# A four-layer graph network on one core: the first layer's attention weights as a third block of the dense builder

## The chip, the cores and the metric

The kernel is written for one NeuronCore of a Trainium2 chip and runs on one core. The metric is the device time of the run in microseconds. A core has TensorE (matrix products, with a separate queue for weight loads), VectorE, ScalarE, GpSimd and SyncE; the last, ScalarE and GpSimd issue DMA transfers.

## The reference, cut to what matters

The graph has 3125 nodes of 64 features and 100,000 edges sorted by target, with a relation type and a weight each. Four layers are applied, each to `relu(layernorm(x))` and added to `x`:

```python
edge_index = stack([src, dst])
h = maximum(layernorm(x), 0);  x = x + L0(h, ..., src, dst, edge_type)
h = maximum(layernorm(x), 0);  x = x + L1(h, edge_index, ...)
h = maximum(layernorm(x), 0);  x = x + L2(h, edge_weight, src, dst)
h = maximum(layernorm(x), 0);  x = x + L3(h, edge_index, ...)

# L0: attention with one head; what is changed is how the last sums are made
e = leaky_relu(concat([h[src], h[dst], emb_rel[etype]]) @ attn_w1 @ attn_w2)
ex = exp(e - segment_max(e, dst)[dst])
a = ex / segment_sum(ex, dst)[dst]
agg = segment_sum(a[:, None] * h[src], dst)
out = relu(where(deg > 0, agg, h) + h @ loop_weight)

# L1: sums of x[dst] @ W_msg over src, by counts of the pairs (src, dst)
# L2: twice  h = segment_sum((h * norm)[src] * w[:, None], dst) * norm
# L3: attention with 8 heads over the edges and one loop per node, then a feed-forward block
```

## The kernel before

Nodes stand as 25 blocks of 125 on 125 partitions (`NB`, `NP`), edges as 784 columns of 128 (`C`, `P`). Node features of a layer are `Hn` (125 x 25 x 64).

**Dense blocks.** Layers L1 and L2 use dense matrices, source by target: for each pair of nodes the number of edges and the sum of their weights. They are built by `dense_block`, one target block of 125 after another, 25 in all. A block's targets are cut into 42 windows of 3 targets, and a window's edges stand in one row of 128; the windows go in 7 parts of 6 (`PARTS`, `QB`). An edge is written as a one-hot row of its source's low digit (0 to 124, `hot(half, 0, W)`, L1651) and a one-hot row of 75 values (`CW`), target in the window times source's high digit (L1650). The second is multiplied by the edge weight, which is split into three bf16 parts, so that their sum keeps fp32 (L1655). TensorE multiplies the first (125 columns as the stationary operand) with counts and first weight part (150 columns, L1096), and with the other two parts (150 columns, L1098), which land in two accumulators. ScalarE copies counts and the first weight accumulator to SBUF (`counts_part`, L799), VectorE adds the second (`weights_part`, L1662, two parts later). Windows with more than 128 edges have overflow rows (26 in all), which `overflow` works off in the second part of the next block: VectorE makes the hot rows, TensorE multiplies (L1108, L1109), VectorE adds into the block (L1687 to L1690). Then ScalarE stores counts and weights (`store`), the counts as whole rows of 12,500 bytes, the weights transposed by target block in pieces of 500 bytes. The two block buffers (`wides`) lie in `big` and `arena`; the first part of a block waits for the stores of the block two before (`blk_out0`, `blk_out1`).

```python
act.dma_start(d_cnt[b], wide_c).then_inc(S[f"blk_out{u}"], 16)
act.dma_start(d_wgt[:, :, b * NP:(b + 1) * NP].rearrange("h p m -> p h m"), ...)
```

**First layer.** GpSimd gathers a feature row for every edge (`tiles`, L652: 784 indirect transfers of 128 rows for L0, and 784 for L3), SyncE stashes them in DRAM in 98 pieces (`stash`), ScalarE reloads these (`reload`). The edge look-up on TensorE and VectorE (L1052 to L1059, L1612 to L1619, 196 steps) gives the scores; `softmax0` scans them into attention weights; the weights go to DRAM (`d_al0`), and GpSimd gathers them as 7 tables (`block_rows`, L658). Then 816 steps follow (`l0_steps`, L989, and L1850): VectorE makes a 128 x 125 matrix of target marks times attention weight, and TensorE multiplies it with 128 gathered rows. Every second step has a filler matmul of 512 columns (L992). `step_targets` and `step_rows` prepare the tables.

**Order.** Histogram of the edges (`hist`: 784 matmuls of 125 columns stationary and 100 streamed, L1029), edge look-up, dense blocks, softmax, steps of L0, counts (L1, L1167 and L1175), two turns of sums (L2), then look-up, softmax, 984 positions of steps and the feed-forward block of L3. Each engine runs its own program in this order and meets the others at semaphores. In a turn of sums the 25 source blocks are read from `d_wgt` by SyncE, and each is multiplied in 7 groups of 500 columns with `T1[:, hi, :]` as the stationary operand (L1196). The result has features on partitions: ScalarE copies it (`sums_out`), TensorE transposes it back in 25 pieces.

## Time and profile before

| | us |
|---|---|
| runs, median of 3 | 3795.6 |
| lowest and highest run | 3776.2, 3814.1 |
| span of the profiled execution | 5607.6 |
| busy in it: TensorE, weight loads | 2765.6, 2175.0 |
| busy: VectorE, ScalarE, GpSimd | 2436.0, 473.0, 1797.6 |
| mean granted TensorE clock in it | 0.614 of 2.4 GHz |

The profiled execution is one execution under the hardware profiler, and here it is much longer than the runs. Every row of the trace comes from it; the change is timed by runs without the profiler. In a table by stretches a row gives start and end, the length, then for TensorE, weight loads, VectorE, ScalarE and GpSimd the busy time with the number of instructions in parentheses, then the granted clock, the share of the DMA engines that was busy, and GB/s. In a timeline a row gives the start, the length, the engine, the line, the operation, output and inputs, and in brackets the idle time before it with what ended it. Rows of the groups by line give the busy time and the mean in ns of one instruction. A matmul's length in the trace overlaps the next one's, so pitches are read from starts.

### The profile page before, as it was taken

To read this page: it belongs to the slowest core of one execution; us is meant where nothing else is said; L and a number is where in the kernel's file an instruction comes from. 1 tells how busy PE (TensorE), PEld (TensorE's weight loads), DVE (VectorE), ACT (ScalarE), POOL (GpSimd) and SP (SyncE) were. 2 spreads that over 40 slices of the span, in tenths; PEclk is the share of its full clock that TensorE was granted. 3 is DMA by queue.
4 is the path that set the end of the run, shared out by engine and by line. 5 is a ranking of instruction groups with operands and counts; after the bars stand their busy time and mean duration, and the time that the engine had idled before them with its cause. 6 is when DMAs were issued, how large, how long until landed. Compare 5 with 4: busy or idle time off the path is not lost.

```text
span 5607.6 us, 46533 instructions
## 1 busy us (share of the span) xinstructions
PE 2765.6 (49%) x14416; PEld 2175.0 (39%) x14458; DVE 2436.0 (43%) x4207; ACT 473.0 (8%) x909; POOL 1797.6 (32%) x1742
## 2 busy tenths in 40 slices
PE   2085022122678885989898500004770001059995
PEld 1083000000157774979733400004660001059983
DVE  4068221111677776970101500006999800035565
ACT  0000000000022331003200100001220110000000
POOL 3705777777100001000000777771000077720000
PEclk8555555555555555989999655557995555555556
DMA  3102222222236665314476121110000123102210
GB/s 109 52 1 61 58 75 62 71 62 65 85 82 140 138 144 155 109 49 160 177 269 220 44 52 49 46 48 10 0 0 23 70 80 73 49 15 66 63 35 23
DMA packets 246489, 433.22 MB, mean 77 GB/s; under 512 B 140538, under 2 KB 142311, under 8 KB 231895
## 3 DMA queue, kind: packets, MB, share of 16 engines
q10 hardware_dynamic: 126001, 172.60, 12.0%
q1 hardware_dynamic: 64102, 198.46, 10.0%
q0 software_dynamic: 56256, 60.51, 5.8%
q8 instruction: 72, 1.18, 0.1%
q14 instruction: 58, 0.48, 0.0%
HBM read 280.32 MB, written 150.98 MB: 77 GB/s over the span
## 4 chain that ended last, share of the span: by engine, by line
PE 35%; issue 25%; another core or an unknown queue 17%; DVE 10%; POOL 9%; DMA 2%; ACT 1%; DVEq 0%; SPq 0%; ACTq 0%; POOLq 0%
POOL ring L652 8%; PE PS L1272 7%; PE PS L1196 5%; PE PS L1096 4%; PE PS L1098 4%; PE PS L989 3%; PE PS L1029 3%; PE PS L1167 3%; PE PS L992 2%; PE PS L1175 1%; DVE s_ring L1612 1%; DVE s_ring L1613 1%; PE PS L1270 1%; PE PS L1290 1%
## 5 line engine op out<-in xcount | busy, mean ns | idle before, releaser
L652 POOL DMA_INDIRECT ring<-d_h,idx_lin x1568 | 1579.1, 1007 | 598.6 <-issue 519.4
L1272 PE MATMUL PS<-arena,s_ring 128*128 x1968 | 432.5, 414 | 198.1 <-issue 198.1
L1096 PE MATMUL PS<-qa 128*125 128x150 bf16 x1050 | 412.3, 393 | 107.0 <-DVE arena L1662 46.1
L1929 DVE TENSOR_TENSOR big<-PS,big 128x800 f32<-128x800 f32 x196 | 193.8, 989 | 619.5 <-issue 335.7
L1272 PEld LDWEIGHTS PS<-arena,s_ring 128*128 128x128 f32 x1968 | 439.8, 330 | 9.2 <-issue 1.1
L1221 PE MATMUL PS<-big 128*125 128x128 bf16 x784 | 134.0, 300 | 618.5 <-issue 449.2
L1098 PE MATMUL PS<-qa 128*125 128x150 bf16 x1050 | 401.2, 382 | 0.0
L1059 PE MATMUL PS<-s_ring,arena 81*128 81x512 bf16 x196 | 121.6, 621 | 561.0 <-issue 353.3
L1221 PEld LDWEIGHTS PS<-big 128*125 128x125 bf16 x784 | 106.9, 209 | 664.8 <-issue 456.6
L671 POOL DMA_INDIRECT d_fa<-asd,start_i x25 | 50.2, 2010 | 889.5 <-DVEq L1323 882.2
L1231 PE MATMUL PS<-big,arena 125*128 125x200 bf16 x2352 | 271.6, 272 | 118.3 <-ACT arena L900 100.9
L1096 PEld LDWEIGHTS PS<-qa 128*125 128x125 bf16 x1050 | 262.5, 250 | 136.0 <-DVE qa L1655 96.0
L1979 DVE TENSOR_TENSOR big<-big,PS 128x512 f32 x123 | 84.6, 688 | 510.1 <-remote 225.3
L1059 PEld LDWEIGHTS PS<-s_ring,arena 81*128 81x128 bf16 x196 | 20.6, 105 | 686.9 <-issue 399.8
L1231 PEld LDWEIGHTS PS<-big,arena 125*128 125x128 bf16 x2352 | 234.7, 111 | 127.7 <-issue 67.8
L1196 PE MATMUL PS<-big,arena 125*64 125x500 f32 (+1 forms) x700 | 267.2, 544 | 25.7 <-DVEq L1323 25.7
L1029 PE MATMUL PS<-s_ring 128*125 128x100 bf16 x784 | 183.3, 411 | 171.4 <-DVE s_ring L1455 110.7
L1098 PEld LDWEIGHTS PS<-qa 128*125 128x125 bf16 x1050 | 264.3, 252 | 0.0
L1850 DVE TENSOR_SCALAR s_ring<-iota_row,arena 128x125 f32<-128x125 f32 x816 | 244.7, 345 | 27.8 <-issue 20.0
L658 POOL DMA_INDIRECT arena<-d_al,tk_i x7 | 6.6, 943 | 773.8 <-DMA d_al<-qa 772.0
L1029 PEld LDWEIGHTS PS<-s_ring 128*125 128x125 bf16 x784 | 180.6, 325 | 173.8 <-DVE s_ring L1455 112.3
L989 PEld LDWEIGHTS PS<-arena,s_ring 128*125 128x125 f32 x1632 | 234.2, 192 | 20.0 <-issue 4.3
(445 smaller groups left out, 4572.2 us busy)
## 6 DMA issues: line engine op xcount, KB each, us to landing
big<-d_wgt SPq DMA_DIRECT2D x50, 1562.5 KB, 7.2
d_stash<-ring SPq DMA_DIRECT2D x196, 256.0 KB
arena<-d_stash ACTq DMA_DIRECT2D x196, 256.0 KB
big<-d_cnt SPq DMA_DIRECT2D x25, 1562.5 KB, 6.5
ring<-d_h,idx_lin POOLq DMA_INDIRECT x1568
d_cnt<-big ACTq DMA_DIRECT2D x13, 1562.5 KB, 5.5
d_wgt<-big ACTq DMA_DIRECT2D x13, 1562.5 KB, 15.7
d_cnt<-arena ACTq DMA_DIRECT2D x12, 1562.5 KB, 5.4
```

The source lines that it names most:

```text
L652: pool.indirect_dma_start(ring[:, HALF * h + s, :], None, table, bass.IndirectOffsetOnAxis(ap=idx_lin[:, CH * i + s:CH * i + s + 1], axis= ...
L989: nc.tensor.matmul(PS[0:NP, bass.ds(to[s], D)], s_ring[:, (j * CH + s) % RING, 0:NP], arena[:, bass.ds(at[s], D)], start=False, stop=False ...
L1029: mm = nc.tensor.matmul(bank(7, NP, 4 * NB), free(s_bf[:, 0:1], [[HALF, NP]], h * W * HALF + s_), free(h_bf[:, 0:1], [[HW * HALF, 4], [HAL ...
L1096: nc.tensor.matmul(bank(3 * half + s // 2, NP, 2 * CW, at), lhs, hot_step(half, s, W, 2 * CW), start=(s % 2 == 0), stop=False, skip_group_ ...
L1098: mm = nc.tensor.matmul(bank(3 * half + s // 2, NP, 2 * CW, at + CW), lhs, hot_step(half, s, W + 2 * CW, 2 * CW), start=False, stop=False, ...
L1167: mm = nc.tensor.matmul(bank(0, NP, D, hi * D), blk_t[:, hi, 0:NP], t_row[:, slot_no, :], start=False, stop=False, skip_group_check=True)
L1196: mm = nc.tensor.matmul(bank(g, D, n), T1[:, hi, :], blk_in[:, slot_no, GW * g:GW * g + n], start=(hi == 0), stop=(hi == NB - 1))
L1221: mm = nc.tensor.matmul(bank(4 + j, NP, P, s * P), free(look_hot[:, 0:1], [[CB, NP]], j * CB * W + s), ident_bf, start=True, stop=True)
L1231: mm = nc.tensor.matmul(bank(2 * j, P, HN, s * (BANK // 2)), look_t[0:NP, j, s * P:(s + 1) * P], src_parts[:, r * HN:(r + 1) * HN], start= ...
L1272: mm = nc.tensor.matmul(PS[:, bass.ds(place[s] + j % SUMS * BANK, D)], marks[:, j % 2, s, :], arena[:, bass.ds(at[s], D)], start=False, st ...
L1850: v_.tensor_scalar(s_ring[:, k % RING, 0:NP], iota_row[:, 0:NP], dstl[:, k:k + 1], alpha0[:, k:k + 1], ALU.is_equal, ALU.mult).then_inc(S[ ...
L1929: v_.tensor_tensor(picked.rearrange("p (s h k) -> p s h k", s=CB, h=H), free(PS[:, 0:1], [[BANK // 2, CB], [NB, H], [1, NB]], 2 * j * BANK ...
```

## The change

The attention weights of L0 become a third block of the dense builder. They are split into three bf16 parts like the edge weights, and each window now has three matmuls with the same stationary operand, now 128 columns wide: the first streams counts, first weight part and first attention part (225 columns), the other two the second and third parts of both (150 columns each), into the same accumulator. VectorE's add goes; ScalarE copies all three quantities. Counts and weights are stored in one transfer, `d_blk[b]`, as whole rows of 25,000 bytes. The attention block stays in SBUF: TensorE multiplies it with `Hn` in 25 fp32 products of 125 x 64 (`agg_products`), five behind each of the last five parts of the next block, and ScalarE copies the sum (`agg_rows`).

So the softmax now stands ahead of the dense blocks, and the attention weights are gathered into the windows' rows (16 gathers, then 16 transposes). The gathers, stash, reloads, tables and steps of L0 go. The blocks now lie with the source on partitions and the target in the columns, so the sums of L2 are made with a slice of the block as the stationary operand: 625 products of 125 x 64 in a turn, whose result needs no copy and no transpose. The histogram's stationary operand, too, has 128 columns.

```diff
-    W = NP + 1
+    W = P
     CW = WN * NB
-    HOT = QB * (W + 4 * CW)
+    HOT = QB * (W + 7 * CW)
...
-        d_cnt = dram("d_cnt", (NB, P, N))
-        d_wgt = dram("d_wgt", (NB, P, N))
-        d_h0 = dram("d_h0", (N, D))
+        d_blk = dram("d_blk", (NB, P, 2 * N))
...
-            nc.gpsimd.memset(arena[:, 0:2 * N], 0.0)
...
-            tiles(0, d_h0, 0, 18)
...
-            tiles(0, d_h0, 18, 40)
+            pool.wait_ge(S["alpha_out"], 16)
+            for g in range(DG):
+                pool.indirect_dma_start(arow[:, g * P:(g + 1) * P], None, d_al0,
+                                        bass.IndirectOffsetOnAxis(ap=tk5_i[:, g:g + 1], axis=0)).then_inc(S["arows_in"], 16)
...
-            block_rows(d_dst, dstl, "drow0_in")
-            tiles(0, d_h0, 40, NCH)
-            pool.wait_ge(S["alpha_out"], 16)
-            block_rows(d_al0, alpha0, "rows_in")
...
-                for q in range(2):
+                for q in range(3):
                     last = nc.scalar.activation(free(blk[:, 0:1], [[NP, NB], [WN, n], [1, WN]], q * N + p * QB * WN),
-                                                free(PS[0:NP, 0:1], [[1, NB], [BANK // 2, n], [NB, WN]], half * 3 * BANK + q * CW), ACT.Copy)
+                                                free(PS[:, 0:1], [[1, NB], [BANK // 2, n], [NB, WN]], half * 3 * BANK + q * CW), ACT.Copy)
...
-                    act.dma_start(d_cnt[bass.ds(2 * i + b, 1)].rearrange("o p m -> p (o m)"), wide_c).then_inc(S[f"blk_out{u}"], 16)
-                    act.dma_start(d_wgt[:, :, bass.ds(2 * NP * i + b * NP, NP)].rearrange("h p m -> p h m"),
-                                  wide_w.rearrange("p (h m) -> p h m", h=NB)).then_inc(S[f"blk_out{u}"], 16)
+                to = d_blk[b] if i is None else d_blk[bass.ds(2 * i + b, 1)].rearrange("o p m -> p (o m)")
+                act.dma_start(to, wides[u][:, 0:2 * N]).then_inc(S[f"blk_out{u}"], 16)
+
+            def agg_rows(i, n):
+
+                act.wait_ge(S["agg_done"], n + 3 if i is None else 2 * i + (n + 3))
...
+                nc.scalar.activation(to, bank(7, NP, D), ACT.Copy).then_inc(S["agg_out"], 1)
...
                 for s in range(QB):
-                    at = s % 2 * (BANK // 2)
-                    lhs = hot_step(half, s, 0, NP)
-                    nc.tensor.matmul(bank(3 * half + s // 2, NP, 2 * CW, at), lhs, hot_step(half, s, W, 2 * CW),
+                    at = half * 3 * BANK + s * (BANK // 2)
+                    lhs = hot_step(half, s, 0, W)
+                    nc.tensor.matmul(PS[:, at:at + 3 * CW], lhs, hot_step(half, s, W, 3 * CW),
                                      start=(s % 2 == 0), stop=False, skip_group_check=True)
-                    mm = nc.tensor.matmul(bank(3 * half + s // 2, NP, 2 * CW, at + CW), lhs, hot_step(half, s, W + 2 * CW, 2 * CW),
-                                          start=False, stop=False, skip_group_check=True)
+                    for r in range(1, 3):
+                        mm = nc.tensor.matmul(PS[:, at + CW:at + 3 * CW], lhs, hot_step(half, s, W + (2 * r + 1) * CW, 2 * CW),
+                                              start=False, stop=False, skip_group_check=True)
...
+            def agg_products(i, n, first, end):
...
+                for hi in range(first, end):
+                    mm = nc.tensor.matmul(bank(7, NP, D), wides[n % 2][0:NP, 2 * N + hi * NP:2 * N + (hi + 1) * NP], Hn[:, hi, :],
+                                          start=(hi == 0), stop=(hi == NB - 1), skip_group_check=True)
...
+                    if p >= 2 and not first:
+                        agg_products(i, b - 1, NB // 5 * (p - 2), NB // 5 * (p - 1))
...
-            l0_steps()
...
-                    for g in range(GROUPS):
-                        n = min(GW, N - GW * g)
-                        mm = nc.tensor.matmul(bank(g, D, n), T1[:, hi, :], blk_in[:, slot_no, GW * g:GW * g + n],
-                                              start=(hi == 0), stop=(hi == NB - 1))
+                    for s in range(NB):
+                        mm = nc.tensor.matmul(bank(0, NP, D, hi * D), blk_in[:, slot_no, s * NP:(s + 1) * NP], T1[:, s, :],
+                                              start=(s == 0), stop=(s == NB - 1))
...
-            for k in range(K):
-                v.wait_ge(S["agg_mm"], k + 1)
-                v_.tensor_scalar(s_ring[:, k % RING, 0:NP], iota_row[:, 0:NP], dstl[:, k:k + 1], alpha0[:, k:k + 1],
-                                 ALU.is_equal, ALU.mult).then_inc(S["s_ready"], 1)
...
+                v_.tensor_tensor(to_w, hits, at_w[:, :, :, bass.ds(k, QB)], ALU.mult)
+                v_.tensor_tensor(to_a, hits, at_a[:, :, :, bass.ds(k, QB)], ALU.mult).then_inc(S["one_ready"], 1)
```

**Order on TensorE, inside the loop of the dense blocks.** Before, the end of one part and the start of the next (L1090 is the wait's register, L1096 and L1098 the two products of a window):

```order
L1096 MATMUL PS<-qa 125x150
L1098 MATMUL PS<-qa 125x150
L1096 MATMUL PS<-qa 125x150
L1098 MATMUL PS<-qa 125x150
L1090 REGISTER_ALU
L1096 MATMUL PS<-qa 125x150
L1098 MATMUL PS<-qa 125x150
L1096 MATMUL PS<-qa 125x150
L1098 MATMUL PS<-qa 125x150
```

After, the same place (L1015 and L1018 are the three products of a window, L1041 those of the attention block):

```order
L1015 MATMUL PS<-qa 128x225
L1018 MATMUL PS<-qa 128x150 x2
L1041 MATMUL PS<-Hn,big 125x64 x5
L1010 REGISTER_ALU
L1015 MATMUL PS<-qa 128x225
L1018 MATMUL PS<-qa 128x150 x2
L1015 MATMUL PS<-qa 128x225
L1018 MATMUL PS<-qa 128x150 x2
```

A third product stands in each window, and five fp32 products stand between two parts.

**Order on VectorE, from the look-up to the first part of the blocks.** Before (L1629 is the last instruction of the placing of overflow rows, L1633 to L1638 split the tables, L1650 begins the hot rows):

```order
L1629 CAST pos_c<-PS 7x128
L1633 CAST big<-qa 128x2048
L1634 TENSOR_SCALAR big<-qa 128x2048
L1636 CAST big<-qa 128x2048
L1638 TENSOR_TENSOR qa<-qa,big 128x2048
L1636 CAST big<-qa 128x2048
L1638 TENSOR_TENSOR qa<-qa,big 128x2048
L1636 CAST big<-qa 128x2048
L1639 CAST qa<-iota_row 128x756
L1650 TENSOR_TENSOR qa<-qa,big 128x450
L1651 TENSOR_TENSOR qa<-qa,big 128x756
L1655 TENSOR_TENSOR qa<-qa,big 128x1350
```

After (L1579 is the last multiply of the softmax, L1675 to L1671 the tables of keys and weights, those with PS the attention weights):

```order
L1579 TENSOR_TENSOR qa<-qa,big 128x784
L1675 CAST s_ring<-qa 128x2048
L1676 TENSOR_SCALAR s_ring<-qa 128x2048
L1669 CAST big<-qa 128x2048
L1671 TENSOR_TENSOR qa<-qa,big 128x2048
L1669 CAST big<-qa 128x2048
L1671 TENSOR_TENSOR qa<-qa,big 128x2048
L1669 CAST big<-qa 128x2048
L1669 CAST qa<-PS 128x2048
L1671 TENSOR_TENSOR qa<-PS,qa 128x2048
L1669 CAST qa<-qa 128x2048
L1671 TENSOR_TENSOR qa<-qa 128x2048
```

The softmax's end now stands ahead of the tables, and five instructions for the attention weights follow them.

**Order on GpSimd, its queue of gathers up to the steps of the last layer.** Before (L652 feature rows, L681 node values to the edge list, L686 rows of the windows, L658 targets and attention weights by step, L700 tables of the last layer):

```order
L652 DMA ring<-d_h,idx_lin 128x64 x144
L681 DMA d_fa<-nfl,start_i 100352x1 x25
L686 DMA big<-d_dense,tk_i 128x384 x16
L652 DMA ring<-d_h,idx_lin 128x64 x176
L658 DMA arena<-d_dst,tk_i 128x128 x7
L652 DMA ring<-d_h,idx_lin 128x64 x464
L658 DMA arena<-d_al,tk_i 128x128 x7
L700 DMA dst<-d_dst,tk_i 128x128 x7
L700 DMA dst<-d_dst,tk_i 88x128
```

After (L643 gathers the attention weights into the windows' rows):

```order
L634 DMA d_fa<-nfl,start_i 100352x1 x25
L639 DMA big<-d_dense,tk_i 128x384 x16
L643 DMA big<-d_al,tk_i 128x128 x16
L652 DMA dst<-d_dst,tk_i 128x128 x7
L652 DMA dst<-d_dst,tk_i 88x128
L627 DMA d_fa<-asd,start_i 100352x8 x25
```

784 gathers of feature rows and 14 tables are gone, and 16 gathers of attention weights stand in their place.

## Rows read from the trace of the kernel before

**Rows 1.** Table by stretches, one row for each stage that is used.

```profile
85.00:298.00 213.00, 38.37 (x161) 35.05 (x160) 14.78 (x34) 3.11 (x7) 137.57 (x144) 0.52 0.27 80
298.00:454.00 156.00, 156.00 (x681) 156.00 (x682) 113.79 (x255) 0.00 (x0) 0.00 (x0) 0.50 0.00 1
...
545.00:1422.00 877.00, 168.38 (x306) 32.81 (x305) 186.52 (x430) 0.00 (x0) 659.70 (x642) 0.50 0.26 67
1422.00:1572.00 150.00, 118.69 (x242) 25.81 (x242) 122.21 (x255) 1.08 (x2) 6.65 (x7) 0.50 0.26 81
...
1594.00:2160.00 566.00, 462.30 (x2152) 432.74 (x2152) 419.06 (x883) 174.06 (x375) 0.00 (x0) 0.50 0.62 136
...
2220.00:2474.00 254.00, 254.00 (x2022) 233.88 (x2021) 244.42 (x816) 1.28 (x1) 0.95 (x1) 0.97 0.32 89
...
2772.00:3060.00 288.00, 275.76 (x745) 101.74 (x745) 11.62 (x9) 6.21 (x14) 0.00 (x0) 0.96 0.71 262
...
3127.00:3836.00 709.00, 97.95 (x644) 79.06 (x644) 88.32 (x118) 23.79 (x40) 515.85 (x504) 0.53 0.19 47
3836.00:4215.00 379.00, 274.36 (x2492) 237.68 (x2492) 351.26 (x471) 93.35 (x156) 0.00 (x0) 0.96 0.00 0
...
4493.00:4931.00 438.00, 40.02 (x180) 36.97 (x183) 17.18 (x24) 16.44 (x16) 334.31 (x331) 0.51 0.25 62
4931.00:5418.00 487.00, 430.55 (x1934) 425.10 (x1972) 243.90 (x346) 0.00 (x0) 13.49 (x13) 0.50 0.15 41
```

**Rows 2.** Groups by line: L1612 in 545:1300 and 1422:1572, L1059 in all.

```profile
L1612 DVE TENSOR_SCALAR s_ring<-arena,tk 125x512 bf16<-125x512 uint8 x44 | 20.9, 476 | 0.0
...
L1612 DVE TENSOR_SCALAR s_ring<-qa,tk 125x512 bf16<-125x512 uint8 x42 | 20.1, 477 | 0.2
...
L1059 PEld LDWEIGHTS PS<-s_ring,arena 81*128 81x128 bf16 x196 | 20.6, 105 | 686.9 <-issue 399.8 <-DVE s_ring L1619 280.9 <-remote 6.2
```

**Rows 3.** Timeline of one part of a dense block, and of its overflow row.

```profile
1802.08 0.39 DVE L1650 TENSOR_TENSOR qa<-qa,big 128x450 bf16<-128x450 bf16 x1
...
1802.38 0.55 DVE L1651 TENSOR_TENSOR qa<-qa,big 128x756 bf16<-128x756 bf16 x1
...
1802.61 0.26 PEld L1096 LDWEIGHTS PS<-qa 128*125 128x125 bf16 x1
...
1802.81 0.25 PEld L1098 LDWEIGHTS PS<-qa 128*125 128x125 bf16 x1
1802.85 0.86 DVE L1655 TENSOR_TENSOR qa<-qa,big 128x1350 bf16<-128x1350 bf16 x1
...
1803.62 0.62 DVE L1662 TENSOR_TENSOR arena<-arena,PS 125x450 f32<-125x450 f32 x1
...
1817.52 0.21 DVE L1664 TENSOR_TENSOR arena<-arena,PS 125x50 f32<-125x50 f32 x1
...
1822.30 0.39 DVE L1650 TENSOR_TENSOR qa<-qa,big 128x450 bf16<-128x450 bf16 x1 [0.49 <-DVE arena L1690]
```

**Rows 4.** Timeline of the tables, and of the hand-over to the steps.

```profile
1582.60 1.23 DVE L1633 CAST big<-qa 128x2048 bf16<-128x2048 f32 x1 [0.17 <-DVE pos_c L1629]
...
1586.38 2.29 DVE L1638 TENSOR_TENSOR qa<-qa,big 128x2048 f32<-128x2048 f32 x1
...
2203.70 0.94 POOL L658 DMA_INDIRECT arena<-d_al,tk_i  x1 [0.30 <-issue]
...
2219.74 2.39 DVE L1850 TENSOR_SCALAR s_ring<-iota_row,arena 128x125 f32<-128x125 f32 x9 [19.98 <-issue]
```

**Rows 5.** Table by stretches of 4 us in the count stage.

```profile
2540.00:2544.00 4.00, 4.00 (x21) 4.00 (x20) 0.00 (x0) 1.01 (x3) 0.00 (x0) 0.50 0.00 0
...
2552.00:2556.00 4.00, 4.00 (x38) 3.92 (x37) 0.00 (x0) 1.60 (x4) 0.00 (x0) 1.00 0.00 0
```

**Rows 6.** DMA issues: KB each, then us to landing; the block stores.

```profile
d_cnt<-big ACTq DMA_DIRECT2D x13, 1562.5 KB, 5.5
d_wgt<-big ACTq DMA_DIRECT2D x13, 1562.5 KB, 15.7
```

## What I expect, and why

> **What bounds the kernel now.** I read the table by stage first, then short timelines inside the stages. The profiled execution lasts 5607.6 us, the runs 3796 us. So something in the trace is not in the runs, and it has to be found before any sum. Four stretches carry it, and in all four GpSimd issues row gathers. In 85 to 298 us TensorE does 161 matmuls; in the next 156 us it does 681 [rows 1]. The edge look-up does 430 VectorE instructions in 877 us, then 255 in 150 us [rows 1]. The look-up of the last layer gets through 40 groups (ScalarE's count) in 709 us, then 156 in 379 us [rows 1]. The last layer's steps: 24 VectorE instructions in 438 us, then 346 in 487 us [rows 1]. At the free pace the four would hold about: 104 histogram matmuls at 0.229 = 24 us; some 84 look-up steps at 3 x 150/255 = 1.76 us or less (short timelines without a gather show less; I take 1.5) plus 60 us of tables = about 185; 40 x 2.43 = 97; and for the last, where the gathers themselves pace the steps, an end some 420 us earlier. Stall: 189 + 692 + 612 + 420 = 1913 us. 5608 - 1913 = 3695 us, 3% below the median of the runs. So I read the stalls as a thing of the profiled execution, nearly absent from the runs, and make the sum against 3796 with the unstalled stretches. What bounds the runs is then a chain of stages: histogram, edge look-up, dense blocks, softmax, the 816 steps, counts, two sums, last layer. The first turn of gathers (784 of about 1.3 us, so 1.0 ms) ran beside look-up and dense blocks, which hold about 0.9 ms with the histogram; it was on no chain of its own by more than a little.
>
> **Removed.** (1) The steps of the first layer, 2220 to 2474 us, TensorE and VectorE both over 95% busy [rows 1]: -254 us. Their gathers, stash stores and reloads were hidden in the runs and go at 0. In the profiled execution they take their two stalls with them, 189 + 692 = 881 us. The other bound: of the 101 us by which my stall-free figure misses the runs, half may be this turn's, so up to -50. (2) The second table set in the middle of the look-up, about 52 small VectorE instructions at some 0.2 us: -10 us.
>
> A page's rule would add a gain. While GpSimd gathers, does it slow VectorE itself? The equality instruction L1612 takes 476 ns on average beside the gathers (545 to 1300 us) and 477 without them (1422 to 1572 us) [rows 2]; I count 0. The Trainium skill ("SBUF — State Buffer", Who interferes with whom) says that VectorE and GpSimd share a port pair by an exclusive lock, held for a whole instruction; by that the look-up's VectorE work would speed up too. The trace does not bear it out for this form.
>
> **Histogram.** The stationary operand goes from 125 to 128 columns. It now runs 681 matmuls in 156 us, 0.229 each, 1.83 us for a step of 8, while VectorE is busy 113.8 us for 85 steps, 1.34 each [rows 1]. Loads of 128 bf16 columns take 105 ns in the trace (81x128, at 1.2 GHz) [rows 2], loads of 125 columns 250 ns [rows 3]. In the dense stage pairs of load and matmul follow each other at 0.20 us although 150 columns stream in 0.125 us at 1.2 GHz [rows 3], so the load sets that pitch. With the short load the histogram becomes VectorE's: 98 x (1.83 - 1.37) = -45 us. Bounds: 0 if the load stays slow, -48.
>
> **Before the blocks.** The softmax (40 us) moves ahead of them whole. From its last multiply to the first step, at 2219.74, VectorE stood idle for 20 us, with 7 gathers of 0.94 + 0.30 us [rows 4]. Now 16 gathers: +11 us; 9 more transposes: +2; three casts of 1.23 and two subtractions of 2.29 for the alpha parts: +8.3 [rows 4]. The tables of keys and edge weights (five of 1.23, two of 2.29, 11 us) now lie behind the gathers: -11; rounding for the last iota, -4. Sum +6 us.
>
> **The blocks, now 566 us** [rows 1], 22.6 us each. VectorE per part: 0.30 + 0.47 + 0.77 start to start for the hot rows [rows 3], and 0.53 for the add, which goes; the second product costs another 0.77. So 2.31 us against 2.07. TensorE per part: 18 pairs instead of 12, 6 x (225 + 150 + 150) = 3150 columns, 2.63 us at 1.2 GHz and 1.31 at 2.4, if loads hide; before, 12 x 0.205 = 2.46. In five of seven parts come 5 fp32 products of 125x64. Such products are two matmuls each (816 steps and 408 fillers are 2040, of which the trace has 2022 [rows 1]); the count stage (125x64 products and transposes, fp32 as well) does 21 matmuls in 4 us at the low clock and 38 at the high one [rows 5], so 0.19 or 0.105 each, 2.0 or 1.05 us per part. The overflow row (one per block, 26 in all) holds VectorE from the last add to 1822.30, about 4.6 us [rows 3]; now TensorE is less behind: 4.2. A block is then
>
> - high clock: VectorE decides, 7 x 2.31 + 4.2 = 20.4 us; 25 of them 510, with a start of 10, 520 us;
> - low clock: TensorE decides, 7 x 2.63 + 25 x 2 x 0.19 + 3.7 of wait after the overflow row = 31.6 us; 790 us, plus 10.
>
> Which clock? Today the stage is at 0.50 with TensorE busy 82% [rows 1], with gaps at every part. The changed one leaves it no gap for five parts of seven at the low clock. The count stage, without gaps, ran at 0.50 from 2520 to about 2548 and then rose [rows 5]; the edge look-up (3 matmuls of 512 columns a step, 79% busy) never rose [rows 1, 5]; the last look-up stayed at 0.96 with 72% busy [rows 1]. I take the rise, with some falling back at the overflow waits: 22.8 us a block, 570 us, +4 us. The whole-row store helps here: 500-byte pieces took 15.7 us, whole rows of the same size 5.5 [rows 6], and ScalarE waited for that store at each block's first part. 3.1 MB in whole rows is about 2 x 5.5 = 11 us, against 11.7 us between its issue and the wait. If it takes 13, VectorE's margin covers half, and the stage grows by some 20 us.
>
> **After the blocks.** The last overflow row, 25 products, two copies and the wait for the last store: +12 us. Then counts as before: their clock fell before them too.
>
> **The two sums.** Both turns take 288 us [rows 1]: 350 matmuls of up to 500 columns each, then ScalarE's copies, transposes and a few VectorE instructions. Now each has 625 products of 125x64, 1250 matmuls at 0.107 = 134 us at the high clock, no copies, no transposes; but such a stream began with 28 us at the low clock (21 matmuls in 4 us [rows 5]), which costs 14. With 6 and 16 us between and behind them, 134 + 14 + 6 + 134 + 16 = 304: +16 us. At the low clock throughout: 1250 x 0.19 = 238, +210 us for both. DMA: 1.56 MB per 5.4 us is the load of today.
>
> **Sum:** -254 - 10 - 45 + 6 + 4 + 12 + 16 = -271. 3796 - 271 = 3525 us, ratio 0.929. In the profiled execution another 881 us go: a span near 4460.
>
> **Rivals.**
> 1. The clock stays low in the blocks: 3525 + 800 - 570 = 3755 us, 1% below before. For it: the edge look-up, bf16 and one-hot rows as here, dense in columns and never up. Against: it uses 81 to 125 rows of the array, and the new blocks hold dense fp32 products. The Trainium skill ("TensorE: Matmul & The Clock Gate", What's actually happening) says that sustained activity releases the throttle; by that this rival falls, but the look-up's 0.50 speaks against a simple reading.
> 2. Slower: the 128-column load is not fast here, where the columns lie 12 bytes apart (in the row of 105 ns they lie side by side). Then 18 pairs at 0.205 are 3.69 us a part; a block 7 x 3.69 + 9.5 + 3.7 = 39 us, 976 us, the histogram saves nothing: 3525 + 406 + 45 = 3976 us. It decides against the change from the pitch at which the blocks use up the 271 us: (841/25 - 13.2)/126 = 0.162 us a pair. If it comes with the high clock, 0.105 a pair gives 1.9 + 1.05 us a part and 3635 us.
> 3. The sums stay at the low clock: 3525 + 194 = 3720 us. For it: the steps of the last layer, 64-column fp32 as well, ran at 0.50 for 487 us. Against: they pause at each step, the count stage did not.
> 4. The change does less than it says: the gathers were co-critical or not, the hand-over is longer, the store is waited for. Upwards 3575, downwards 3470.
>
> **Numbers.** Forecast as summed 0.57; its own range, with the dense stage between 520 and 640 and the 50 us, 3440 to 3610. Rival 1: 0.14. Rival 2 at the low clock 0.10, at the high one 0.04. Rival 3: 0.07. Rival 4: 0.08, inside the first range. Range 3440 to 3790, which leaves out rival 2 and what lies below. A measurement of this kernel tells about 1% from no change. Faster by over 1% (under 3758): 0.57 + 0.08 + 0.07 + 0.04 and most of half of rival 1, less what each may miss: 0.77. Within 1%: 0.11. Slower: 0.12.
>
> **What would show it.** No stall in the histogram and the edge look-up, which takes about 300 us in one piece. Histogram steps of 1.37 us. Loads of 128 columns near 0.11 us in the blocks and in the histogram. Blocks of 20 to 24 us with a granted clock mostly at 1.0; at 0.50 they would be near 32. No wait of ScalarE for the block store. The sums at 134 to 150 us each with the clock at 1.0 after the first 30 us. If blocks take over 33 us, or sums over 230, the forecast is wrong in that term; if the runs fall by far more than 300 us, the first turn's gathers cost the runs what I gave to the profiled execution alone.

## The result, and the profile of the changed kernel

The change made the kernel slower: 4266.5 us (median of 4 runs, 4257.1 to 4274.8) against 3792.1 (4 runs, 3776.2 to 3814.1), ratio 1.126 with an interval of 1.121 to 1.131. I had forecast 3525 us.

One fact has to stand ahead of the comparison. A job is a set of kernels that were run together on one chip, the kernel before always among them, and the jobs are of two kinds: in one the kernel before takes about 3790 us in every run, in the other about 5600. The execution of [rows 1] is of the second kind, so the stalls that I read out of it do not come from the profiler. They do not follow the chip's number either: chip 3 had stalls (two jobs) and chip 10 had none, but number 2 stands for a job with stalls and, four minutes later, for one without. The profile of the changed kernel (span 4263.3 us) has no stalls. A stall-free profile of before came out of an experiment: the kernel before without the first turn of gathers, 3784.4 us there, ratio 0.9985 to before. Its stages are the ones to compare with.

The table by stretches of the changed kernel (start:end, length, then busy time and count of TensorE, weight loads, VectorE, ScalarE, GpSimd, then granted clock, DMA share, GB/s): histogram, edge look-up, dense blocks, counts, the two sums, the last layer from its gathers on.

```profile
102.00:256.00 154.00, 153.53 (x781) 105.28 (x780) 130.59 (x292) 0.00 (x0) 0.00 (x0) 0.50 0.00 1
321.00:637.00 316.00, 284.02 (x587) 62.90 (x585) 300.96 (x648) 0.00 (x0) 20.23 (x14) 0.50 0.32 99
741.00:1832.00 1091.00, 994.84 (x4411) 655.08 (x4412) 462.12 (x876) 254.64 (x570) 0.00 (x0) 0.50 0.16 70
1904.00:2115.00 211.00, 211.00 (x1884) 208.94 (x1884) 0.00 (x0) 93.08 (x197) 0.00 (x0) 1.00 0.47 167
2136.00:2667.00 531.00, 524.71 (x2500) 524.54 (x2500) 11.62 (x9) 0.00 (x0) 0.00 (x0) 0.50 0.39 142
2708.00:4263.00 1555.00, 943.50 (x5828) 838.68 (x5827) 1077.45 (x1151) 171.45 (x272) 979.80 (x867) 0.67 0.24 66
```

The same view of the kernel before without its first gathers, stall-free; its fourth row is the steps of the first layer:

```profile
102.00:282.00 180.00, 179.85 (x784) 179.61 (x784) 130.95 (x296) 0.00 (x0) 11.21 (x128) 0.50 0.11 43
345.00:702.00 357.00, 286.05 (x587) 63.13 (x587) 324.27 (x714) 0.00 (x0) 131.41 (x661) 0.50 0.44 149
733.00:1290.00 557.00, 461.04 (x2148) 432.07 (x2149) 414.65 (x869) 173.03 (x372) 0.00 (x0) 0.50 0.58 137
1358.00:1608.00 250.00, 250.00 (x2036) 230.91 (x2035) 242.59 (x812) 1.28 (x1) 0.00 (x0) 0.99 0.31 90
1664.00:1883.00 219.00, 218.86 (x1892) 216.60 (x1890) 0.10 (x1) 93.79 (x198) 0.00 (x0) 0.96 0.44 161
1903.00:2184.00 281.00, 272.08 (x723) 97.41 (x724) 11.62 (x9) 3.11 (x7) 0.00 (x0) 0.97 0.73 268
2232.00:3785.00 1553.00, 931.10 (x5787) 838.41 (x5828) 1078.41 (x1151) 171.49 (x272) 978.57 (x867) 0.67 0.23 66
```

| from | before | after | difference | forecast |
|---|---|---|---|---|
| histogram | 180 | 154 | -26 | -45 |
| end of histogram to first dense product (look-up; softmax now in it) | 451 | 485 | +34 | +56 |
| dense blocks | 557 | 1091 | +534 | +4 |
| from there to the counts (softmax and steps, now the last products) | 374 | 72 | -302 | -302 |
| counts | 219 | 211 | -8 | 0 |
| two sums, to the last layer | 349 | 593 | +244 | +16 |
| last layer | 1553 | 1555 | +2 | 0 |

The differences add up to +478 us, the spans (3785.9 and 4263.3) differ by 477. The forecast's column adds up to its -271. The 60 us of softmax and hand-over leave the fourth row (-254 - 60 + 12 = -302) and come into the second (-10 + 60 + 6 = +56). The dense blocks and the sums took 778 us more between them where I had 20. Of the other terms, the histogram gained 19 us less than forecast, and the look-up's row came out 22 us better: the look-up itself gained 41 us (316 instead of 357) where I had counted 10, and what follows it took back a part.

A part of a dense block in the changed kernel, rows of its timeline (start, length; several instructions in one row have their count behind x):

```profile
1240.61 0.48 PE L1015 MATMUL PS<-qa 128*128 128x225 bf16 x1
...
1240.91 0.59 PE L1018 MATMUL PS<-qa 128*128 128x150 bf16 x2
...
1241.32 0.48 PE L1015 MATMUL PS<-qa 128*128 128x225 bf16 x1
1241.32 0.13 PEld L1018 LDWEIGHTS PS<-qa 128*128 128x128 bf16 x1
...
1242.74 2.18 PE L1041 MATMUL PS<-Hn,big 125*125 125x64 f32 x10
...
1243.06 0.39 DVE L1691 TENSOR_TENSOR qa<-qa,s_ring 128x450 bf16<-128x450 bf16 x1 [3.83 <-PE PS L1018]
...
1244.71 0.48 PE L1015 MATMUL PS<-qa 128*128 128x225 bf16 x1
...
1248.97 2.19 PE L1041 MATMUL PS<-Hn,big 125*125 125x64 f32 x10
```

The load is short, as forecast (0.13 us against 0.25 [rows 3]). Still 225 columns take 0.30 us and 150 take 0.20, so a window takes 0.71 us: 1.33 ns a column where 1.2 GHz would need 0.83. A part is six windows and ten matmuls of the attention block, 4.26 + 1.97 = 6.23 us. VectorE waits 3.83 us in each, and a block takes 1091 / 25 = 43.6 us.

### The profile page after: what moved, and what is told of

It is laid out like the page before. It is cut to its first block, busy times and chain, and to the rows that moved or that the text cites. A ratio compares the mean times of both kernels' runs of the same rounds, so it can differ in the third digit from the quotient of the medians.

```text
span 4263.3 us, 48040 instructions
## 1 busy us (share of the span) xinstructions
PE 3222.3 (76%) x16493; PEld 2491.6 (58%) x16494; DVE 2219.0 (52%) x3326; ACT 545.1 (13%) x1092; POOL 1078.1 (25%) x959
## 4 chain that ended last, share of the span: by engine, by line
PE 53%; POOL 23%; DVE 10%; issue 9%; DMA 3%; ACT 1%; SPq 0%; DVEq 0%; ACTq 0%; POOLq 0%
POOL ring L614 20%; PE PS L1109 12%; PE PS L1018 10%; PE PS L1015 7%; PE PS L1041 6%; PE PS L931 4%; PE PS L1081 3%; PE PS L1182 2%; PE PS L1089 2%; DMA qa<-d_code 2%; PE PS L954 1%; POOL nmx L620 1%; DVE arena L1877 1%; POOL d_fb L627 1%; PE PS L955 1%
## 5 line engine op out<-in xcount | busy, mean ns | idle before, releaser
L614 POOL DMA_INDIRECT ring<-d_h,idx_lin x784 | 850.7, 1085 | 250.7 <-issue 250.7
L1018 PE MATMUL PS<-qa 128*128 128x150 bf16 x2100 | 616.1, 383 | 0.0
L1015 PE MATMUL PS<-qa 128*128 128x225 bf16 x1050 | 505.7, 482 | 105.7 <-DVE qa L1697 105.7
L1109 PE MATMUL PS<-arena,big 125*125 125x64 f32 x2500 | 525.5, 416 | 26.3 <-DVEq L1233 20.0
L1109 PEld LDWEIGHTS PS<-arena,big 125*125 125x125 f32 x2500 | 525.1, 332 | 26.5 <-DVEq L1233 26.5
L1018 PEld LDWEIGHTS PS<-qa 128*128 128x128 bf16 x2100 | 270.4, 129 | 248.8 <-issue 176.3
L652 POOL DMA_INDIRECT dst<-d_dst,tk_i x8 | 7.6, 950 | 1171.6 <-DVEq L1233 1169.5
L1015 PEld LDWEIGHTS PS<-qa 128*128 128x128 bf16 x1050 | 148.5, 141 | 183.0 <-DVE qa L1697 99.9
L1822 DVE TENSOR_REDUCE qa<-big 128x800 f32 x196 | 193.2, 986 | 28.3
L749 ACT ACTIVATE big<-PS 128x450 f32<-128x450 f32 (+1 forms) x273 | 128.9, 548 | 497.4 <-PE PS L1018 497.4
L749 ACT ACTIVATE arena<-PS 128x450 f32<-128x450 f32 (+1 forms) x252 | 119.1, 549 | 406.0 <-PE PS L1018 406.0
L954 PE MATMUL PS<-s_ring,arena 125*81 125x512 bf16 x196 | 127.5, 650 | 54.6 <-DVE s_ring L1520 53.9
```

What stands on the lines that cost most here:

```text
L614: pool.indirect_dma_start(ring[:, HALF * h + s, :], None, table, bass.IndirectOffsetOnAxis(ap=idx_lin[:, CH * i + s:CH * i + s + 1], axis= ...
L749: last = nc.scalar.activation(free(blk[:, 0:1], [[NP, NB], [WN, n], [1, WN]], q * N + p * QB * WN), free(PS[:, 0:1], [[1, NB], [BANK // 2, ...
L1015: nc.tensor.matmul(PS[:, at:at + 3 * CW], lhs, hot_step(half, s, W, 3 * CW), start=(s % 2 == 0), stop=False, skip_group_check=True)
L1018: mm = nc.tensor.matmul(PS[:, at + CW:at + 3 * CW], lhs, hot_step(half, s, W + (2 * r + 1) * CW, 2 * CW), start=False, stop=False, skip_gr ...
L1109: mm = nc.tensor.matmul(bank(0, NP, D, hi * D), blk_in[:, slot_no, s * NP:(s + 1) * NP], T1[:, s, :], start=(s == 0), stop=(s == NB - 1))
L1822: v_.tensor_reduce(qa[:, bass.ds(CB * H * g, CB * H)], picked.rearrange("p (s k) -> p s k", k=NB), AX_X, ALU.add).then_inc(S["look_sum"], 1)
```

## Experiments

Stage times are first to last product of the stage; only they are compared between jobs. Whole times are compared within one job. The kernels of the last two parts (both remedies, the stalls) ran 4 to 10 times in a job, and their times are medians; each of the others ran once. What the expectations call a chip with or without stalls is a job of that kind. Line numbers are each kernel's own; the first matmul of a window is the one that streams 225 columns.

**The streamed operand side by side.**

```diff
+            return free(hots[:, 0:1], [[1, n]], h * HOT + at * QB + j * n)
...
-                    nc.tensor.matmul(PS[:, at:at + 3 * CW], lhs, hot_step(half, s, W, 3 * CW),
+                    nc.tensor.matmul(PS[:, at:at + 3 * CW], lhs, hot_stream(half, s, W, 3 * CW),
```

> The changed kernel, with one thing other: the streamed operand of the three products of a window is read from neighbouring columns (2 bytes apart) instead of columns 12 bytes apart. What is streamed is then not the window's own columns, so the dense blocks hold other numbers. Theory A (the stream of columns 12 bytes apart sets the pitch: in the profile of the changed kernel 150 columns take 0.20 us and 225 take 0.30, 1.33 ns a column, at a granted clock of 0.50): pitches fall to 0.125 and 0.19 us at 1.2 GHz, a part's 18 matmuls from 4.23 to about 2.7 us, the dense stage from 1117 to about 850 us, the time from 4267 to about 4000. Theory B (the load of the stationary operand sets the pitch, as my forecast had it for 125 columns): no change, 4267 within 1%. If the clock rises as well, the stage falls below 700 us.

Measured: dense stage 593 us at a clock of 0.81, in a job with stalls. Theory A held, and the clock rose too, with TensorE busy only 81% of the time. The row of the stage, then a window where the clock stood at 1.00, in which 225 columns take 0.10 us, 0.44 ns each:

```profile
741.00:1334.00 593.00, 481.20 (x4413) 458.54 (x4414) 461.12 (x875) 255.27 (x570) 0.00 (x0) 0.81 0.30 130
```

```profile
999.87 0.26 PE L1018 MATMUL PS<-qa 128*128 128x225 bf16 x1
999.97 0.29 PE L1021 MATMUL PS<-qa 128*128 128x150 bf16 x2
```

**The stationary operand side by side** (`lhs` read with step 1 instead).

> The changed kernel with the stationary operand (not the streamed one) of the windows' products read from neighbouring columns; the blocks then hold other numbers. Read by the dense stage, first to last product (1091 us in the changed kernel, 593 with the streamed operand side by side). Theory A (the stream's 12-byte steps set the pitch): still 1091 us, pitches 0.20 and 0.30 us. Theory B (loads count too): shorter pitches, a stage under 1050 us. TensorE's granted clock stays at 0.50 by A.

Measured: 1084 us at 0.50, 4268.2 us in all (before 3795.6 beside it). The step of the loads costs next to nothing here.

```profile
744.00:1828.00 1084.00, 987.91 (x4411) 649.21 (x4412) 462.02 (x875) 255.09 (x570) 0.00 (x0) 0.50 0.17 71
```

**Other steps of the streamed operand** (2 or 4 elements instead of 6 in `hot_step`'s place).

> The changed kernel with the streamed operands read at other steps: 4 bytes for the 225 columns and for the first 150, 8 bytes for the second 150; the blocks then hold other numbers. If a column costs 0.111 ns for each byte of step, as 1.33 ns at 12 bytes would have it, 4 bytes cost 0.44 ns and the clock sets the pitch (0.42 or 0.83 ns a column), and 8 bytes cost 0.89 ns: 0.133 us for 150 columns at either clock. If instead any step above 2 bytes costs the same, the pitches stay at 0.30 and 0.20 us and the stage at 1091 us. By the first the stage is near 600 us with the clock at 0.8 or above.

Measured: 595 us at 0.92, 3769.3 us in all. The table row, then two windows of the timeline at the high clock:

```profile
744.00:1338.00 594.00, 496.32 (x4407) 483.56 (x4405) 460.93 (x874) 255.91 (x570) 0.00 (x0) 0.92 0.30 129
```

```profile
1020.39 0.28 PE L1018 MATMUL PS<-qa 128*128 128x225 bf16 x1
1020.51 0.37 PE L1021 MATMUL PS<-qa 128*128 128x150 bf16 x2
1020.70 0.29 PE L1018 MATMUL PS<-qa 128*128 128x225 bf16 x1
```

At 4 bytes 225 columns take 0.12 us, 0.53 ns each, not far from the 0.44 of neighbouring columns. The two of 150, one at 4 and one at 8 bytes, take 0.19 to 0.20 together, so the one at 8 bytes takes about 0.12, an estimated 0.8 ns a column. Steps of 12 bytes cost 1.33 ns. In the changed histogram, where the columns lie 16 bytes apart, eight loads of 128 columns go by in 1.28 us with products of 100 columns between them, about 1.6 ns a column if the stream is what holds them there, which no run tested. From 8 bytes on the cost grows about with the distance, some 1.6 to 1.8 ns for each 16 bytes passed. The Trainium skill ("SBUF — State Buffer", Door 1: The DMA port swizzle, the note on cachelines) says that SBUF has lines of 16 bytes, that each access to a new line costs, and that two hits on a line are enough for full bandwidth. The steps of 12 bytes agree with that; the step of 8 bytes, two hits on a line, does not, with about 0.8 ns a column at the high clock. I had not weighed that rule. By it the stream of [rows 3] would have been a rival to the load for what sets the pitch of 0.20 us.

**A filler matmul behind each window.**

```diff
+                    mm = nc.tensor.matmul(bank(3 * half + s // 2, P, BANK), ones_bf[:, 0:P], zero_bf[:, 0:BANK], start=False, stop=False, skip_group_check=True)
```

> The changed kernel with one more matmul behind the three of each window: 512 columns of zeros with ones as the stationary operand, added to the window's own bank, so the result stays. Theory A (the clock is low in the blocks because the stream is too thin, and more streamed columns raise it): granted clock 1.0, a part's PE work (4.23 + 6 x 0.43) / 2 = 3.4 us or less, the dense stage about 28 us a block, 700 us, the time about 3850. Theory B (the clock stays at 0.50 whatever TensorE streams here, as in the edge look-up of the first layer): a part grows by 6 x 0.43 = 2.6 us, the stage by 450 us, the time to about 4720.

Measured: neither. The clock rose to 0.94, as theory A said, but the stage took 1217 us, 126 more than without fillers. Table row, then the timeline where the clock stood at 1.00 (L1021 is the filler):

```profile
741.00:1959.00 1218.00, 1115.03 (x5360) 659.00 (x5461) 462.94 (x877) 255.03 (x570) 0.00 (x0) 0.94 0.15 63
```

```profile
1247.41 0.46 PE L1015 MATMUL PS<-qa 128*128 128x225 bf16 x1
1247.69 0.59 PE L1018 MATMUL PS<-qa 128*128 128x150 bf16 x2
1248.10 0.40 PE L1021 MATMUL PS<-zero_bf,ones 128*128 128x512 bf16 x1
1248.33 0.46 PE L1015 MATMUL PS<-qa 128*128 128x225 bf16 x1
```

The streams 12 bytes apart take 0.28 us for 225 columns and 0.205 for 150 at the high clock too, against 0.30 and 0.205 at the low one. So twice the clock hardly changes their pace; only fillers and fp32 products went faster. The high clock alone would not have given the forecast's 20.4 us a block.

**Without the products of the attention block** (24 of 25 left out).

> The changed kernel without 24 of the 25 fp32 products of each attention block (the first layer's sums are then missing). A block has 240 fewer matmuls at 0.22 us each for pairs: 24 x 0.44 = 10.6 us a block if TensorE alone sets the pace, 265 us of the stage's 1091. If their place were covered by VectorE's work: under 50 us. The clock stays at 0.50 if the windows' stream decides it; if the fp32 products hold it down, it rises.

Measured: 862 us at 0.50, so -229 us; 4037.0 us in all. TensorE paces alone, and these products cost 24 x 2 x 0.19 = 9.1 us a block. They did not hold the clock down.

```profile
742.00:1604.00 862.00, 766.15 (x3269) 418.60 (x3267) 461.42 (x874) 255.47 (x570) 0.00 (x0) 0.50 0.21 89
```

**The kernel before, streamed operand side by side.**

> The kernel before with the streamed operand of its dense blocks read side by side (the blocks then hold other numbers). My forecast took the load of 125 columns for what sets the pitch of 0.20 us. If that was right: pitch and clock stay, the dense stage stays near 557 us. If the 12-byte step set it there too: pitch down to what load and 150 columns allow (0.125 us at the low clock if loads hide), TensorE's part 1.5 to 1.9 us, VectorE sets the pace, stage 510 to 540 us, granted clock up if TensorE then streams densely enough.

Measured: 518 us instead of 557, clock 0.50 in both, pitch 0.175 us instead of 0.20. The row of the stage and two starts, 0.17 us apart:

```profile
1593.00:2111.00 518.00, 395.44 (x2147) 376.98 (x2147) 410.92 (x870) 172.89 (x372) 0.00 (x0) 0.50 0.62 147
```

```profile
1805.74 0.38 PE L1101 MATMUL PS<-qa 128*125 128x150 bf16 x1
...
1805.91 0.38 PE L1099 MATMUL PS<-qa 128*125 128x150 bf16 x1
```

Both views were partly right. The 12-byte step set 0.20. What is left, 0.175, is more than the 0.125 of 150 columns at 1.2 GHz, and the load of 125 columns is the likely reason; no run changed it. VectorE, busy for 411 of the 518 us, kept the gain small.

**The roles in the sums swapped back.**

```diff
-                        mm = nc.tensor.matmul(bank(0, NP, D, hi * D), blk_in[:, slot_no, s * NP:(s + 1) * NP], T1[:, s, :],
+                        mm = nc.tensor.matmul(bank(hi // 4, D, NP, hi % 4 * NP), T1[:, s, :], blk_in[:, slot_no, s * NP:(s + 1) * NP],
```

> The changed kernel with the roles in the two sums swapped back: T1 (64 columns) is the stationary operand, each 125 x 125 slice of a block is streamed, ScalarE copies the seven banks and TensorE transposes the 25 pieces, as before. Theory A (64 streamed fp32 columns behind a load of 125 keep the clock low; 125 streamed behind a load of 64 raise it): granted clock near 1.0, both turns about 300 us instead of 500, the time about 4065. Theory B (the low clock comes from what ran before or from the small pieces as such): clock 0.50; 78125 columns at the low clock are 270 us a turn, the time about 4300.

Measured: 287 us for both turns, clock 0.97. Theory A held, and what ran before the sums was the same. The same 2500 matmuls (and 25 transposes), with 125 columns streamed behind loads of 64 instead of 64 behind loads of 125:

```profile
2144.00:2431.00 287.00, 278.08 (x2525) 277.52 (x2524) 11.62 (x9) 3.11 (x7) 0.00 (x0) 0.97 0.72 263
```

**Fillers in the sums**, one of 512 columns behind every fifth product, then behind each.

> The changed kernel with a filler matmul of 512 bf16 columns (into a bank that nobody reads) behind every fifth product of the two sums, 250 in all. Theory A (more streamed columns raise the clock): 134 + 125 x 0.21 = 161 us a turn at the high clock, both about 340 us instead of 500, the time about 4110. Theory B (it doesn't): 250 x 0.43 = 107 us more, the time about 4375.

> The changed kernel with a filler matmul of 512 bf16 columns behind every product of the two sums (1250; with one behind every fifth the clock stayed at 0.50 and the sums took 611 us). If more streamed columns raise the clock: near 1.0, and a turn is 1250 x 0.107 + 625 x 0.21 = 267 us, both about 550. If the clock stays low: 1250 x 0.20 + 625 x 0.43 = 519 us a turn, both about 1060.

Measured: 611 us at 0.50 with 250 fillers, 492 us at 0.99 with 1250 (532 at 0.50 without). The two rows:

```profile
2137.00:2748.00 611.00, 605.00 (x2750) 580.48 (x2751) 11.67 (x10) 0.00 (x0) 0.00 (x0) 0.50 0.34 124
```

```profile
2136.00:2629.00 493.00, 486.55 (x3751) 446.83 (x3751) 11.75 (x10) 0.00 (x0) 0.00 (x0) 0.99 0.42 154
```

TensorE is busy 99% of the time in all three, so the busy time of a profile does not tell which clock was granted. With 250 fillers the clock stayed low and they cost 79 us; with 1250 it rose, and the stage was 40 us shorter although it held more work. The Trainium skill ("TensorE: Matmul & The Clock Gate", What's actually happening) says that activity releases the throttle; read as the busy time of a profile, that does not hold here (524.71 of 531 us busy at 0.50).

**Hot rows in pairs.** VectorE writes the streamed rows so that the windows of a pair stand side by side; a step's columns are then 4 bytes apart.

```diff
-            return free(hots[:, 0:1], [[QB, n]], h * HOT + at * QB + j)
+            return free(hots[:, 0:1], [[2, n]], h * HOT + j // 2 * HG + at * 2 + j % 2)
```

> The changed kernel with the hot rows laid out in pairs of windows: a step's columns are 4 bytes apart instead of 12; all results as in the reference. VectorE writes runs of two instead of six elements, and makes six multiplications of 450 elements a part instead of two of 1350. If the step is the cause and 4 bytes are short enough: TensorE's part falls as with neighbouring columns, the dense stage to 600 to 660 us (VectorE's part is 0.30 + 0.47 + 6 x 0.30 = 2.57 us if runs of two keep its rate), clock at 0.8 or above. If VectorE loses its rate in short runs: 3918 elements at about 1 ns, 4.2 us a part, 30 a block, 820 us.

Measured: 644 us at 0.85, 3822.2 us in all (before 3795.6). The blocks hold the right numbers here, so the gain of the run with neighbouring columns did not come from its other numbers. In this kernel a slip of naming also took another row of constants in the last layer's layer norm; no stage read here is touched by it, and the later kernels are without it. At the low clock 225 columns 4 bytes apart take 0.19 us, 0.83 ns each, so there the clock sets the pace again:

```profile
1004.88 0.39 PE L1018 MATMUL PS<-qa 128*128 128x225 bf16 x1
...
1005.07 0.46 PE L1021 MATMUL PS<-qa 128*128 128x150 bf16 x2
```

VectorE's multiplications keep their rate in runs of two (0.30 us for 450 elements), its two comparisons do not quite: 462 and 670 ns on average instead of 394 and 552.

**Both remedies.** Pairs and swapped roles; then with the stationary rows left in runs of six.

> The changed kernel with both remedies, all results as in the reference: hot rows in pairs of windows (columns of the streamed operand 4 bytes apart) and T1 as the stationary operand of the two sums. If the two causes are independent, the dense stage is 644 us (1091 in the changed kernel) and the sums 287 (532): 4267 - 447 - 245 = 3575 us, ratio to the kernel before 0.94. If one remedy only moves the wait, it is above 3700.

> As the kernel with both remedies, but only the streamed rows are laid out in pairs; the stationary ones stay in runs of six, columns 12 bytes apart, where VectorE writes them in 0.47 us instead of 0.57. If the stationary operand's step costs TensorE nothing (the run with side-by-side loads says so), VectorE's 0.10 us in each of 175 parts is gained: 17 us less than with all rows in pairs, about 3560. If it costs at the high clock: no gain, or a loss.

Measured, in a job with stalls: 4530.4 us, ratio 0.8075 (0.804 to 0.811), and 4513.5 us, 0.8046 (0.801 to 0.808). Dense stage 669 and 648 us, sums 287 in both. The gain of the second over the first, 17 us, is the expected one, but the intervals overlap, and the dense stage of the first took 669 us here and 644 in the run before it with the same code for the blocks (clock 0.81 and 0.85). A difference of 20 us in such a stage shows nothing.

> The kernel with both remedies and only the streamed rows in pairs, once more. On the chip without stalls the stage times (dense blocks 648, sums 287 us, against 1091 and 532 of the changed kernel) give 4267 - 443 - 245 = 3579 us, ratio to the kernel before 0.944. On the chip with stalls: 4513 us, 0.805, as before.

> The kernel with both remedies (streamed rows in pairs, T1 as the stationary operand of the sums), for the chip without stalls: 4267 - 443 - 245 = 3579 us, ratio 0.944. If the job falls on the chip with stalls: 4515 us, 0.805, as twice before.

Measured: 4522.3 us, 0.8063 (0.804 to 0.809) with stalls; without them 3580.7 us, ratio 0.9472 (0.9448 to 0.9496) to the kernel before at 3785.6. So the version with both remedies beats the kernel before in both kinds of jobs, and the changed kernel too (5209.0 us beside the 4522.3, and 1.126 to before where this one has 0.947). Its dense stage and sums without stalls:

```profile
742.00:1384.00 642.00, 492.18 (x4414) 466.48 (x4415) 515.65 (x1571) 254.90 (x570) 0.00 (x0) 0.84 0.28 120
1686.00:1973.00 287.00, 277.94 (x2525) 277.48 (x2525) 11.62 (x10) 3.11 (x7) 0.00 (x0) 0.97 0.72 263
```

**The stalls.**

> The changed kernel, unaltered. On the chip with stalls: the runs of this kernel with one thing altered there (4970 us with 245 us less in the sums, 5331 with 126 more in the blocks, 5283 with 79 more in the sums) give 5204 to 5215 us, so the change is FASTER there than the kernel before, ratio 0.93. On the chip without stalls 4267 us, ratio 1.125. By the rival (the stalls have nothing to do with the gathers that the change removes) the ratio is about 1.1 on both.

> The kernel before with the 784 gathers of the first layer left out (each is a small GpSimd memset of zeros; stash, reloads and steps stay, so the first layer's sums are zero). On the chip without stalls my forecast has the gathers hidden: 3795 us within 50. If they slow the look-up or the blocks there: 100 us or more less. On the chip with stalls: two stalls of 189 and 692 us go, 5600 - 881 = about 4720 us.

> The kernel before without the first layer's 784 gathers, for the chip without stalls: 3795 us within 50 if they are hidden there, as the forecast had it; 3700 or less if they slow the look-up and the blocks. On the chip with stalls: 4733 us, as before.

Measured: in a job with stalls the changed kernel takes 5209.0 us, ratio 0.930 (0.927 to 0.933), so there the same change is a gain. The kernel before without its first gathers takes 4733.2 us there, 871 less than 5604.3 (expected 881), and 3784.4 against 3785.6 without stalls. The look-up of the last layer in the changed kernel, first in a job with stalls, then without:

```profile
3000.00:3100.00 100.00, 8.00 (x44) 5.98 (x44) 4.62 (x6) 1.79 (x3) 75.73 (x74) 0.50 0.18 51
```

```profile
3000.00:3100.00 100.00, 73.00 (x674) 63.14 (x674) 93.31 (x127) 25.13 (x42) 74.63 (x78) 0.98 0.20 52
```

GpSimd gathers at the same pace in both; TensorE gets through 44 matmuls where it otherwise does 674. What the engines wait for is not shown (the waits name "issue" and "remote", up to 45 us each). What makes one job stall and another not stays open: with number 2 in both kinds, the runs do not show that it is the chip, although the expectations name it so.

## Why the forecast was wrong

**What held.** That the stalls hang on the gathers, and their size: 881 us for the first turn, and 4733 us shows 871. I had them as a thing of the profiled execution, though, and they are in every run of some jobs. That the gathers cost nothing without stalls: ratio 0.9985. The upper bound of 50 us for them was not needed. Steps, softmax and hand-over: -302 us where I had -302. The short load of 128 columns. The store: 8.8 us for 3.1 MB, and ScalarE waits for TensorE, not for it.

**The step that failed first** is the sentence on the pitch: 150 columns stream in 0.125 us at 1.2 GHz, "so the load sets that pitch". The 0.20 us fitted both a load of 0.25 us that overlaps, and a stream that is slow by itself. I took the one without asking what else could give it, although the columns' distance stood in the code and I used it in the slower rival, on the wrong operand. With 1.33 ns a column a part is 3150 x 1.33 = 4.2 us at either clock, where I had 2.63 or 1.31. That is 7 x 1.6 = 11 us a block above my low-clock case, 280 us in all. The runs show this step wrong: with the stream side by side and the loads as they were the stage fell from 1091 to 593 us, with the loads side by side it stayed at 1084.

**The second is the clock**, in the blocks and in the sums. I took its rise in the count stage as a sign for any dense fp32 stream. The sums ran at 0.50 for 532 us with TensorE 99% busy, and the dense stage for 1091 us with 91%. The count stage was no such stream by itself. It holds a transpose of 125 streamed columns for every two matmuls of 64:

```profile
L1167 PE MATMUL PS<-big 125*125 125x64 f32 x1208 | 157.3, 276 | 0.0
L1175 PE MATMUL PS<-ident,big 125*125 125x125 f32 x615 | 97.6, 292 | 0.0
```

The new sums have the matmuls of 64 alone, and with 125 columns streamed instead they ran at 0.97. Whether the transposes are what let the count stage rise was not tested.

Rival 1 and rival 3 came true together, and I had priced each alone: 800 - 570 = 230 us and 194 us. With the stream's 280 that is 704 us; measured were 530 + 228 = 758 beyond the forecast for the two stages. Most of the rest lies in the sums, where a matmul took 0.21 us (2500 in 524.71) and not 0.19, which makes 50 us.

**Rival 2 had the right shape and the wrong cause.** It put a pair at 0.205 us from a slow load and gave 39 us a block, 3976 us. The measured products of 150 columns do stand 0.20 us apart, those of 225 stand 0.30, and the load is fast.

**The histogram** gained 26 us of 45. VectorE decides, as forecast, but a step takes 1.57 us (154 / 98), not 1.37:

```profile
104.94 0.69 DVE L1363 TENSOR_TENSOR s_ring<-big 128x1024 bf16<-128x1024 bf16 x1
...
106.38 1.30 PEld L931 LDWEIGHTS PS<-s_ring 128*128 128x128 bf16 x8 [0.18 <-DVE s_ring L1365]
106.64 0.69 DVE L1363 TENSOR_TENSOR s_ring<-big 128x1024 bf16<-128x1024 bf16 x1 [0.31 <-PE PS L931]
...
108.11 0.69 DVE L1363 TENSOR_TENSOR s_ring<-big 128x1024 bf16<-128x1024 bf16 x1
```

VectorE's steps stand 1.47 us apart when it waits for nothing (106.64 to 108.11); my 1.37 came from its busy time of 1.34. Before every second step it waits another 0.31 us for TensorE. This is read from the rows; no run changed it.

**The chances.** The range left the result out by 477 us. The forecast counted the clock's two rivals as separate, small ones, but both hang on one question, which clock a stream of short fp32 products gets, and the rows did not favour the answer that I took. In [rows 1] such streams stood at 0.97 in the first layer's steps, which have a filler of 512 columns at every second step, and at 0.50 in the last layer's steps; the counts, at 1.00, have their transposes.

## What to carry to other kernels

Before a matmul's pitch is put down to its load, divide it by the streamed columns and look at how far apart these lie: at 12 bytes a column cost about 1.3 ns at either clock, at 4 bytes 0.83 at the low and 0.53 at the high one. When a change cuts streams into shorter ones behind larger loads, price it at the low clock too: the same product with roles swapped ran at 0.97 instead of 0.50 and took 287 us instead of 532. And when a profiled execution is half as long again as the runs, look whether other runs of the same kernel are too, before it is put down to the profiler; here one change was a loss of 13% in one kind of job and a gain of 7% in the other.

## What the runs showed of the hardware beyond that

Streaming 225 columns that lie 12 bytes apart takes 0.30 us at a granted clock of 0.50 and 0.28 at 1.00. TensorE busy for 91% of a stage or more went together with a clock of 0.50 (blocks and sums) as well as with 1.00 (counts) and 0.99 (sums with 1250 fillers). And in the jobs with stalls the other engines nearly stood still while GpSimd issued row gathers: TensorE was busy for 8 of 100 us instead of 73, with the gathers at an unchanged pace of 1.25 us each.
